# Retiming the loads of the next batch's adjacency matrix in a four-layer graph network

## The chip, the cores and the metric

The kernel runs on one core of one Trainium2 chip. The metric is the device time of one execution in microseconds (us); lower is better. All arithmetic is in 32-bit floats.

## What is computed

Eight independent batches `b`, each with node features `x[b]` (2048 x 128) and an adjacency matrix `adj[b]` (2048 x 2048, 16 MB), pass through four layers. Each layer adds its result to `x`; its input is `h = relu(layernorm(x))`. Cut to what matters:

```
# layer 0: three graph convolutions on h
for i in range(3):
    h = relu(layernorm(adj^T @ (h @ Ws[i]) + bs[i] + h) * gammas[i] + betas[i])
# layer 1: additive attention, softmax over j of sum_d a[d]*relu(q[j,d] + k[i,d]), masked where adj == 0
# layer 2: four-head dot attention, masked by (1 - adj) * -1e9
# layer 3: normalised propagation
A1 = adj + eye(2048);  d = rsqrt(sum(A1, axis=-1))
x = x + ((A1 * d[:, None] * d[None, :]) @ h) @ B
```

Every layer needs the whole of `adj[b]`.

## The kernel before, in words

A batch is cut into 16 tiles of 128 rows; a tile of `adj` is 128 x 2048 floats, 1 MB. Batches are done one after the other, and each in four stages that follow the layers. All engines run their own programs and meet on semaphores.

**Where `adj` lives.** Layer 0 uses it three times, so it is held whole in on-chip memory, in `A` (`adj_res`, line 147), 16 tiles. This memory is the same that layers 1 and 2 use for their own buffers (lines 148 to 165), so `A` of the next batch can only be loaded in the last stage of the batch before, when those buffers are no longer in use. Layers 1, 2 and 3 read `adj` again through a small ring of two tiles, `ring` (`adj_ring`, line 93), one slot for even and one for odd tiles; each tile is loaded anew in each of the three stages. The ring loads are issued by SyncE (line 301), which waits for each slot on `ring_free`.

**Who loads `A`.** POOL does, in `batch(b, more)` (lines 346 to 364), one transfer of 1 MB per tile with line 350, at the head of its program for the batch. Each load of batch b waits on the semaphore `hb_sb` for a tile of the last stage of batch b-1. For batch 0 there is no earlier batch, so ScalarE raises `hb_sb` by 16 at the start (line 493), and all sixteen waits pass. Behind the loads stand the small LayerNorm steps of POOL (`rstd_step`, lines 325 to 332). Tiles 0 to 7 raise `adj_in[0]` and tiles 8 to 15 `adj_in[1]`.

**The last stage (layer 3), lines 1169 to 1197.** TensorE goes through the 16 tiles in eight pairs, 0 to 7. For a pair:

- it transposes both ring tiles in 16 blocks each into PSUM (L1177), after VectorE has added the identity to each tile's diagonal block (`self_loops`, L766), which in turn waits for the ring load;
- ScalarE and VectorE copy the transposed blocks out (L374, L778) into `AGG` and `HT`;
- it multiplies them with `H`, first the even tile, then the odd one (L1189; 32 instructions a tile, since a 32-bit matmul is issued as two). The first of these for each tile raises `ring_free`, and SyncE issues the next pair's load into that slot;
- ScalarE copies each tile's product out (`evac(hbT...)`, line 565), and this raises `hb_sb` by one. That is the event on which the loads of `A` wait;
- a last small matmul (L1197) and an update of `X` (L786) end the pair.

The waits of this cycle that matter in code:

```
1187    pe.wait_ge(o3_rdy, T + (NT + 2))
1191    if j == 0:
1192        last.then_inc(ring_free, 1)
 565    evac(hbT[:, u, :], ps[:, 6 + u, 0:P]).then_inc(hb_sb, 1)
```

So in each pair there are up to four transfers of 1 MB: two into the ring for the next pair, and the loads of `A` released by this pair's two tiles. The last pair has no ring load after it. In the last batch's last stage there is no load of `A` at all.

**The next batch's first stage.** TensorE starts layer 0 with the first half of `A` for all four column chunks (`aggregate`, L1001, 64 instructions), after a wait for `adj_in[0]`, and then takes the second half after a wait for `adj_in[1]` (line 1115). Within the second half it calls `project` (L986), which needs ScalarE's copy of the chunk (`evac_agg`, L374). ScalarE begins the batch with twelve row sums over the tiles of `A` for the degrees (`degrees`, L424), with the same two waits ahead of tile 0 and tile 8 (line 421), and comes to `evac_agg` after them. SyncE first issues the store of the result of the batch before (L305), waits for it, and then issues sixteen loads of 64 KB into `X` (L293) and the first ring load of the batch. `X` is read in the third graph convolution (line 857 and below).

Of the kernel before, what the change touches and what calls it, by code (L numbers as in the profile page):

```python
# [12 lines left out]
NT = N // P  # L13
# [47 lines left out]
def e_lag(u, m):  # L61

    return 2 if u * QUADS + m - TURN in (0, 1) else EQ


class Steps:
# [13 lines left out]
def build(nc, x, adj, Ws, bs, gammas, betas, W1, W2, a_vec, Wq, bq, Wk, bk, Wv, bv, Wo, bo, Bw, out):  # L80
# [4 lines left out]
    with ExitStack() as ctx:  # L85
# [3 lines left out]
        def sem(name):  # L89
            return ctx.enter_context(nc.semaphore(name))  # L90
# [155 lines left out]
        hb_sb = sem("hb_sb")  # L246
# [66 lines left out]
        @block.gpsimd  # L313
        def _(pool):
            pool.memset(ident[:, :], 0.0).then_inc(pool_self, 1)
            pool.memset(halves[:, :], -0.5).then_inc(pool_self, 1)
            pool.memset(epses[:, :], LN_EPS).then_inc(pool_self, 1)
            pool.memset(ones[:, :], 1.0).then_inc(pool_self, 1)
            pool.wait_ge(pool_self, 4)
            pool.affine_select(out=ident[:, :], in_=ident[:, :], compare_op=ALU.not_equal, fill=1.0, base=0,  # L320
                               pattern=[[-1, P]], channel_multiplier=1).then_inc(id_rdy, 1)
            own = Steps(pool_self, LN_COUNT + 1)
            own.k = 4

            def rstd_step(b, k):

                over = LN_STEPS[k][1]
                t = slice(over[0], over[-1] + 1)
                pool.wait_ge(ln_stats, b * LN_COUNT + k + 1)
                own.done(pool.tensor_tensor(var[:, t], mv[:, t, 1], epses[:, t], ALU.add))  # L330
                own.wait(pool, b)
                pool.tensor_tensor(rstd[:, t], var[:, t], halves[:, t], ALU.pow).then_inc(ln_rstd, 1)

            def fetch(b):

                pool.dma_start(HW[:, :].rearrange("p (t d) -> p t d", t=NT),
                               x_v[bass.ds(b, 1)].rearrange("o p t d -> p (o t) d")).then_inc(xn_in, 16)

            def fetched_rstd(b):

                pool.wait_ge(xn_stats, b + 1)
                nc.gpsimd.tensor_tensor(xvar[:, :], xmv[:, :, 1], epses[:, :], ALU.add).then_inc(xvar_rdy, 1)
                pool.wait_ge(xvar_rdy, b + 1)
                nc.gpsimd.tensor_tensor(xrstd[:, :], xvar[:, :], halves[:, :], ALU.pow).then_inc(xn_rstd, 1)

            def batch(b, more):
                own.k = 4
                for t in range(NT):
                    pool.wait_ge(hb_sb, b * NT + t + 1)
                    pool.dma_start(A[:, t, :], adj_v[bass.ds(b, 1), t].rearrange("o p n -> p (o n)")).then_inc(adj_in[t // HALF], 16)  # L350
                for k in range(LN_EARLY):
                    rstd_step(b, k)

                pool.wait_ge(deg_rdy, (b + 1) * NT)
                own.done(pool.tensor_tensor(deg1[:, :], deg[:, :], ones[:, :], ALU.add))
                own.wait(pool, b)
                pool.tensor_tensor(dinv[:, :], deg1[:, :], halves[:, :], ALU.pow).then_inc(dinv_rdy, 1)
                for k in range(LN_EARLY, LN_MID):
                    rstd_step(b, k)
                pool.wait_ge(qk2_dve, b * 2 + 1)  # L360
                fetch(b + 1 if more else b)
                fetched_rstd(b + 1)
                for k in range(LN_MID, LN_COUNT):
                    rstd_step(b, k)

            fetch(0)
            fetched_rstd(0)
            for b in range(NB):
                batch(b, b < NB - 1)

        @block.scalar
        def _(act):
# [61 lines left out]
            def quad(T, m, u, first):  # L434
                if not (first and m < EQ):
                    act.wait_ge(e_used, T * QUADS + (m - e_lag(u, m) + 1))
                s = e_slot(u, m)
                nc.scalar.activation(E[:, s + 2, SPLIT:N], Q2[:, SPLIT:N], ACT.Relu, bias=ka[:, u, 32 + m:33 + m])  # L438
                nc.scalar.activation(E[:, s + 3, :], Q2[:, :], ACT.Relu, bias=ka[:, u, 48 + m:49 + m]).then_inc(e_act, 1)  # L439
# [129 lines left out]
        def _(dve):  # L569
# [104 lines left out]
            def quad(T, m, u, first):  # L674
                if not (first and m < EQ):
                    dve.wait_ge(e_used, T * QUADS + (m - e_lag(u, m) + 1))
                s = e_slot(u, m)
                nc.vector.tensor_scalar(E[:, s, :], Q2[:, :], kd[:, u, m:m + 1], 0.0, ALU.add, ALU.max)  # L678
                nc.vector.tensor_scalar(E[:, s + 1, :], Q2[:, :], kd[:, u, 16 + m:17 + m], 0.0, ALU.add, ALU.max)  # L679
                nc.vector.tensor_scalar(E[:, s + 2, 0:SPLIT], Q2[:, 0:SPLIT], kd[:, u, 32 + m:33 + m], 0.0,  # L680
                                        ALU.add, ALU.max).then_inc(e_dve, 1)
# [538 lines left out]
```

## Time and profile before

| what | value |
|---|---|
| time, median of 3 runs | 13284.21 us (13282.43 to 13297.99) |
| the profiled execution | 13291.54 us |
| its span | 13289.7 us |
| TensorE matmul busy | 12572.4 us, 95% of the span |
| VectorE busy | 9769.1 us, 74% |
| ScalarE busy | 9628.7 us, 72% |
| POOL busy | 351.3 us, 3% |
| mean granted TensorE clock | 0.972 of full speed |
| moved by the DMA engines | 647.66 MB, mean 49 GB/s |
| ring loads | 384 of 1 MB, median 4.9 us from issue to landing |
| loads of `A` | 128 of 1 MB, median 7.4 us |

The span is the time from the first to the last instruction of the profiled execution. An engine's busy time is the union of its instructions. The chain that ended last is found by going back from the last instruction, at each step to what released it; a microsecond saved on an engine counts only where that chain runs through it. A batch takes about 1656 us, of which the last stage is some 100 us.

### The profile page before, as it was taken

The page shows a single profiled execution, that of the slowest core. Times are in us where ns is not written, and L with a number is a line of the kernel's source. Part 1 is how long each engine was busy: PE and PEld are TensorE (multiplying, and loading weights), DVE is VectorE, ACT ScalarE, POOL GpSimd, SP SyncE. Part 2 cuts the span into 40 slices and gives each one's busy share as a digit, 9 for nine tenths or more (in the row PEclk, how much of TensorE's full clock was granted, in tenths as well). Part 3 has the DMA queues.
Part 4 walks back from the last instruction along what each step waited for, and adds up shares of the span by engine and source line. Part 5 has one row for each costly group of instructions (what it writes and reads, how often), then busy time and mean ns, then how long its engine had stood idle before and what let it go on. Part 6 is the DMA issues. An engine that isn't in the chain of part 4 may idle for free.

```text
span 13289.7 us, 251470 instructions
## 1 busy us (share of the span) xinstructions
PE 12572.4 (95%) x110721; PEld 6215.5 (47%) x110721; DVE 9769.1 (74%) x13975; ACT 9628.7 (72%) x8953; POOL 351.3 (3%) x500
## 2 busy tenths in 40 slices
PE   8998999989999899998999989999899998999989
PEld 3333843338433384333843338433384334843348
DVE  4887748877488774887758877588765887658876
ACT  4886748867488664886648866488664886658866
POOL 1000000000000000000000000000000000000000
PEclk9999999999999999999999999999999999999999
DMA  1001210012100121001310013100130001300022
GB/s 71 17 20 45 100 60 17 20 45 104 56 17 20 48 105 52 17 20 48 110 47 18 19 48 117 40 20 17 52 122 32 20 17 52 129 25 20 17 55 87
DMA packets 126941, 647.66 MB, mean 49 GB/s; under 512 B 15264, under 2 KB 49824, under 8 KB 52128
## 3 DMA queue, kind: packets, MB, share of 16 engines
q1 hardware_dynamic: 92688, 420.78, 9.4%
q0 software_dynamic: 20880, 143.66, 2.9%
q10 hardware_dynamic: 12288, 67.13, 2.2%
q8 instruction: 879, 14.40, 0.4%
q14 instruction: 206, 1.69, 0.0%
HBM read 556.01 MB, written 8.39 MB: 42 GB/s over the span
## 4 chain that ended last, share of the span: by engine, by line
PE 88%; DVE 6%; ACTq 2%; DMA 2%; ACT 1%; issue 1%; POOL 0%; SPq 0%; DVEq 0%
PE ps L1017 50%; PE ps L1001 10%; PE ps L1059 8%; PE ps L1072 4%; PE ps L1030 4%; PE ps L1050 3%; PE ps L1189 3%; ACTq L540 2%; PE ps L953 2%; DMA adj_ring<-in_adj 1%; PE ps L1177 1%; DVE E L678 1%; DVE E L679 1%; DVE PT L705 1%; DVE stats L604 1%
## 5 line engine op out<-in xcount | busy, mean ns | idle before, releaser
L1017 PE MATMUL ps<-E,a_win 128*32 128x512 f32 x65536 | 7128.7, 594 | 46.4 <-ACT E L439 34.9
L1017 PEld LDWEIGHTS ps<-E,a_win 128*32 128x32 f32 x65536 | 2114.9, 110 | 4879.7 <-issue 4737.3
L439 ACT ACTIVATE E<-Q,ka 128x2048 f32<-128x2048 f32 x2048 | 4073.1, 1989 | 0.0
L678 DVE TENSOR_SCALAR E<-Q,kd 128x2048 f32<-128x2048 f32 x2048 | 2631.1, 1285 | 1016.5 <-PE ps L1017 982.4
L438 ACT ACTIVATE E<-Q,ka 128x1280 f32<-128x1280 f32 x2048 | 2786.7, 1361 | 810.9 <-PE ps L1017 786.0
L679 DVE TENSOR_SCALAR E<-Q,kd 128x2048 f32<-128x2048 f32 x2048 | 2623.9, 1281 | 0.0
L746 DVE CUSTOM_DVE_ANT_0 T<-ps,adj_ring 128x2048 f32<-128x2048 f32 x512 | 1173.5, 2292 | 231.9 <-PE ps L1050 205.3
L680 DVE TENSOR_SCALAR E<-Q,kd 128x768 f32<-128x768 f32 x2048 | 1258.8, 615 | 0.0
L464 ACT ACTIVATE T<-T,nmin 128x2048 f32<-128x2048 f32 x512 | 1022.0, 1996 | 319.4 <-issue 199.3
L374 ACT ACTIVATE PT<-ps 128x512 f32<-128x512 f32 x1792 | 999.7, 594 | 287.3 <-PE ps L1059 275.4
L1059 PE MATMUL ps<-ident,T 128*128 128x128 f32 x8192 | 1129.8, 281 | 10.1 <-ACT PT L374 5.9
L1059 PEld LDWEIGHTS ps<-ident,T 128*128 128x128 f32 x8192 | 886.3, 142 | 219.2 <-issue 201.2
L374 ACT ACTIVATE AGG<-ps 128x512 f32<-128x512 f32 x224 | 127.7, 596 | 1095.8 <-PE ps L1001 979.7
L1001 PE MATMUL ps<-adj_res,H 128*128 128x512 f32 x2048 | 889.5, 592 | 0.0
L1050 PE MATMUL ps<-kst,qcur 128*128 128x512 f32 x2048 | 624.7, 428 | 267.7 <-DMA kst<-kl 224.5
L1072 PE MATMUL ps<-PT,V 128*32 128x128 f32 x16384 | 658.5, 279 | 0.0
L1001 PEld LDWEIGHTS ps<-adj_res,H 128*128 128x128 f32 x2048 | 384.2, 190 | 459.2 <-issue 459.2
L1030 PEld LDWEIGHTS ps<-H,PT 128*128 128x128 f32 x4096 | 476.8, 195 | 110.6 <-issue 110.6
L1050 PEld LDWEIGHTS ps<-kst,qcur 128*128 128x128 f32 x2048 | 360.4, 197 | 329.1 <-issue 241.9
L1030 PE MATMUL ps<-H,PT 128*128 128x128 f32 x4096 | 501.0, 282 | 7.0 <-DVE PT L705 7.0
L753 DVE COPY PT<-ps 128x512 f32<-128x512 f32 x512 | 353.0, 690 | 178.8 <-PE ps L1059 178.2
L1001 PE MATMUL ps<-adj_res,HW 128*128 128x512 f32 x1024 | 447.3, 595 | 32.5 <-DMA adj_res<-in_adj 32.5
(119 smaller groups left out, 7558.4 us busy)
## 6 DMA issues: line engine op xcount, KB each, us to landing
adj_ring<-in_adj SPq DMA_DIRECT2D x384, 1024.0 KB, 4.9
adj_res<-in_adj POOLq DMA_DIRECT2D x128, 1024.0 KB, 7.4
qst<-qh ACTq DMA_DIRECT2D x64, 256.0 KB, 7.9
qst<-ql ACTq DMA_DIRECT2D x64, 256.0 KB, 9.0
kst<-kh ACTq DMA_DIRECT2D x64, 256.0 KB, 5.7
kst<-kl ACTq DMA_DIRECT2D x64, 256.0 KB, 5.9
HW<-in_x POOLq DMA_DIRECT2D x9, 1024.0 KB, 13.3
X<-in_x SPq DMA_DIRECT2D x128, 64.0 KB, 2.0
```

The source lines that it names most:

```text
L438: nc.scalar.activation(E[:, s + 2, SPLIT:N], Q2[:, SPLIT:N], ACT.Relu, bias=ka[:, u, 32 + m:33 + m])
L439: nc.scalar.activation(E[:, s + 3, :], Q2[:, :], ACT.Relu, bias=ka[:, u, 48 + m:49 + m]).then_inc(e_act, 1)
L678: nc.vector.tensor_scalar(E[:, s, :], Q2[:, :], kd[:, u, m:m + 1], 0.0, ALU.add, ALU.max)
L679: nc.vector.tensor_scalar(E[:, s + 1, :], Q2[:, :], kd[:, u, 16 + m:17 + m], 0.0, ALU.add, ALU.max)
L680: nc.vector.tensor_scalar(E[:, s + 2, 0:SPLIT], Q2[:, 0:SPLIT], kd[:, u, 32 + m:33 + m], 0.0, ALU.add, ALU.max).then_inc(e_dve, 1)
L746: nc.vector.tensor_tensor_reduce(out=T2[:, h, :], in0=ps[:, 0:4, :].rearrange("p c n -> p (c n)"), in1=ring[:, u, :], scale=1.0, scalar=BI ...
L1001: last = mm(ps[:, c, :], src[:, t, :], A[:, t, c * CH:(c + 1) * CH], start=(t == 0), stop=(t == NT - 1))
L1017: last = mm(ps[QROWS * grp:QROWS * (grp + 1), 4 * u + c, :], win, E[:, s + grp, c * CH:(c + 1) * CH], start=(m == 0), stop=(m == QUADS - 1 ...
L1030: last = mm(ps[:, 4 * u, 0:D], PT1[:, j * P:(j + 1) * P], H[:, j, :], start=(j == 0), stop=(j == NT - 1))
L1050: last = mm(ps[:, c, :], qcur[:, u, h, :], kst[:, h, c * CH:(c + 1) * CH], start=True, stop=True)
L1059: last = nc.tensor.transpose(ps[:, 4 + g % 2, k * P:(k + 1) * P], T2[:, h, j * P:(j + 1) * P], ident[:, :])
L1072: last = mm(ps[HD * k:HD * (k + 1), 6 + h % 2, 0:P], V[:, g * TPC + k, h * HD:(h + 1) * HD], PT2[:, g, k * P:(k + 1) * P], start=(g == 0), ...
```

## The change

A table names for each tile `t` of the next batch's `A` the tile of the last stage whose `hb_sb` count releases its load. Before, that was tile `t` itself.

```diff
 def e_lag(u, m):
 
     return 2 if u * QUADS + m - TURN in (0, 1) else EQ
+
+
+LOAD_AFTER = (0, 1, 3, 4, 6, 8, 9, 11, 12, 13, 14, 14, 15, 15, 15, 15)
 
 
 class Steps:
@@ -346,7 +349,7 @@
             def batch(b, more):
                 own.k = 4
                 for t in range(NT):
-                    pool.wait_ge(hb_sb, b * NT + t + 1)
+                    pool.wait_ge(hb_sb, b * NT + LOAD_AFTER[t] + 1)
                     pool.dma_start(A[:, t, :], adj_v[bass.ds(b, 1), t].rearrange("o p n -> p (o n)")).then_inc(adj_in[t // HALF], 16)
                 for k in range(LN_EARLY):
                     rstd_step(b, k)
```

Load 2 now waits for tile 3, load 3 for tile 4, and so on; the six loads 10 to 15 wait for tiles 14, 14, 15, 15, 15 and 15, the tiles of the last pair. Nothing else differs. In the profile of the changed kernel, all line numbers below line 63 are higher by 3.

## Rows read from the trace of the kernel before

**Rows 1.** The page, chain that ended last: shares of the span by line

```profile
PE ps L1017 50%; PE ps L1001 10%; PE ps L1059 8%; PE ps L1072 4%; PE ps L1030 4%; PE ps L1050 3%; PE ps L1189 3%; ACTq L540 2%; PE ps L953 2%; DMA adj_ring<-in_adj 1%; PE ps L1177 1%; DVE E L678 1%; DVE E L679 1%; DVE PT L705 1%; DVE stats L604 1%
```

**Rows 2.** Busy table, the eight last stages: length, engines, PEclk, DMA share, GB/s

```profile
1604.40:1709.10 104.70, 93.66 (x769) 90.95 (x770) 30.47 (x73) 22.54 (x53) 8.29 (x16) 0.95 0.79 289
3262.50:3365.60 103.10, 93.00 (x769) 89.75 (x770) 30.24 (x74) 22.48 (x53) 8.35 (x16) 0.96 0.80 294
4916.70:5022.90 106.20, 96.24 (x769) 93.35 (x770) 30.70 (x73) 22.55 (x53) 8.30 (x16) 0.92 0.78 285
6577.90:6675.60 97.70, 91.01 (x769) 87.79 (x770) 30.15 (x73) 22.34 (x53) 8.31 (x16) 0.98 0.85 310
8230.10:8327.90 97.80, 92.43 (x769) 89.37 (x770) 30.38 (x73) 22.39 (x53) 8.26 (x16) 0.97 0.84 310
9882.30:9986.20 103.90, 93.88 (x769) 90.90 (x770) 30.48 (x73) 22.50 (x53) 8.25 (x16) 0.95 0.80 292
11541.20:11636.80 95.60, 91.11 (x769) 87.77 (x770) 30.22 (x73) 22.33 (x53) 8.32 (x16) 0.98 0.87 317
13188.70:13283.80 95.10, 90.53 (x768) 87.56 (x768) 30.20 (x73) 22.09 (x52) 0.00 (x0) 0.98 0.46 155
```

**Rows 3.** The chain in order of time, last stage of batch 0: start, length, what

```profile
1662.18 10.10 DMA adj_ring<-in_adj
```

**Rows 4.** The same in the last stage of the last batch

```profile
13206.34 6.20 DMA adj_ring<-in_adj
...
13230.64 7.68 DMA adj_ring<-in_adj
```

**Rows 5.** Line 301 in the last stages of batch 0 and of the last batch

```profile
DMA to landing us min/median/max: 4.7/5.1/10.1
...
DMA to landing us min/median/max: 4.7/4.9/7.7
```

**Rows 6.** Busy table by pair, batch 0 (first two) and last batch

```profile
1617.70:1634.60 16.90, 12.61 (x102) 12.18 (x101) 4.50 (x11) 3.14 (x7) 1.06 (x2) 0.93 0.78 299
1646.70:1658.20 11.50, 11.36 (x102) 11.06 (x101) 4.15 (x11) 3.03 (x7) 1.06 (x2) 1.00 0.95 336
...
13215.10:13226.80 11.70, 11.56 (x102) 11.37 (x103) 4.21 (x11) 3.03 (x7) 0.00 (x0) 1.00 0.54 181
13226.80:13240.90 14.10, 11.62 (x102) 10.98 (x100) 4.09 (x11) 3.03 (x7) 0.00 (x0) 1.00 0.43 150
```

**Rows 7.** Busy table at the start of the program, first batch's loads of A

```profile
30.00:40.00 10.00, 0.00 (x0) 0.00 (x0) 0.96 (x2) 0.00 (x0) 2.09 (x5) 1.00 1.01 425
...
60.00:70.00 10.00, 10.00 (x25) 4.45 (x24) 0.00 (x0) 6.31 (x7) 0.00 (x0) 1.00 0.59 246
```

**Rows 8.** DMA queues from 13229 to 13238: packets, MB, share of 16 engines

```profile
q8 instruction: 1, 0.02, 0.7%
```

**Rows 9.** Line 350, whole program: duration ns min/median/max, first and last start

```profile
L350 POOL DMA_DIRECT2D adj_res<-in_adj x128: 530/530/617, 23.6 to 11636.5; - x128
...
DMA to landing us min/median/max: 4.9/7.4/35.3
```

**Rows 10.** Turn from batch 0 to 1: timelines of POOL, SyncE; chain; L424; ScalarE

```profile
1705.28 0.53 POOL L350 DMA_DIRECT2D adj_res<-in_adj  x1 [9.04 <-ACT hbT L374]
1708.86 0.53 POOL L350 DMA_DIRECT2D adj_res<-in_adj  x1 [3.04 <-ACT hbT L374]
...
1709.52 0.40 SPq L305 DMA_DIRECT2D out_x<-X  x1
...
1709.10 36.05 PE ps L1001 x84
...
L424 ACT ACTIVATE adj_ring<-adj_res x12: 1901/1909/1912, 1708.8 to 1731.2; 128x2048 f32<-128x2048 f32 x12
...
1743.48 0.60 ACT L374 ACTIVATE AGG<-ps 128x512 f32<-128x512 f32 x1 [10.29 <-PE ps L1001]
```

**Rows 11.** Timeline of POOL in pair 4 of batch 0's last stage

```profile
1662.54 0.53 POOL L350 DMA_DIRECT2D adj_res<-in_adj  x1 [7.53 <-ACT hbT L374]
```

## The prediction, made before the changed kernel was run

> **What bounds the kernel now.** I read the page's chain of work first. Nine of its fifteen named shares are lines of TensorE, L1017 alone with half of the span; the only transfer of any weight is the ring load, `adj_ring<-in_adj`, at 1% [rows 1]. So the change can touch only short stretches in which the chain leaves TensorE for a ring load. `adj_res`, which the change retimes, is not named there. The first batch's loads are left alone by the change: all their waits are satisfied from the outset.
>
> Second, the busy table over the last stage of each batch, from its first L1189 to the next batch's first L1001 [rows 2]. This is the best view here, because the kernel holds its own control: the last batch has no next one, so its stage runs without any of the sixteen loads of A. It takes 95.1 us with the DMA engines 0.46 busy. The other seven take 95.6 to 106.2 us at 0.78 to 0.87, and add up to 709.0 us (104.7 + 103.1 + 106.2 + 97.7 + 97.8 + 103.9 + 95.6). Seven times 95.1 is 665.7. **43.3 us in the whole program** go with the loads of A, 6.2 us a batch on average, 0.4 to 11.1 in a single one.
>
> Third, the chain inside such a stage. In batch 0 it leaves TensorE three times for a ring load, each issued with the second tile of a pair, at worst for 10.10 us [rows 3]. The same chain in the last batch still leaves twice, for 6.20 and 7.68 us [rows 4]. All fourteen ring loads there land in 4.7 to 7.7 us, median 4.9, and in batch 0 in 4.7 to 10.1, median 5.1 [rows 5]. So a ring load of about 5 us is hidden, each microsecond above it is paid, and the median ring load does not suffer from A; the long ones do.
>
> Fourth, pair by pair [rows 6], each stretch from one pair's first L1189 to the next's: pairs 1 and 3 of batch 0, pairs 2 and 3 of the last. An undisturbed pair takes 11.5 or 11.7 us, whether it moves 336 GB/s (batch 0) or 181 (the last). A disturbed one takes 16.9 with A's loads, 14.1 without. A pair of before asks for two ring loads and two of A, 4 x 1.049 MB = 4.19 MB in 11.5 us, or 365 GB/s; with the first batch's loads in flight the core got 425 GB/s [rows 7]. It runs at 86% of what it can have, so a lagging DMA engine makes up its lag slowly. I take a stall's size as that lag plus what else stands in its queue. What starts it is there without A as well: during the last batch's long ring load, issued at 13230.64, one 16 KB packet of the instruction queue went out [rows 4, 8]. The change does not remove that.
>
> **The change, part by part.** It removes and adds no instruction. The same 128 `adj_res` loads are issued by POOL, 0.53 us each [rows 9]; only the tile whose `hb_sb` count releases each of them moves. Before, two loads go with every pair. After, by pairs 0 to 7: 2, 1, 1, 1, 2, 1, 2, 6. Pairs 0 to 6, in which ring loads are in flight, issue 10 instead of 14.
>
> *Last stage.* Pairs that ask for 4.19 MB fall from seven to three (0, 4 and 6); the other four ask for 3.15 MB, 274 GB/s in 11.5 us, 64% of 425. Sharing the 43.3 us evenly over seven pairs, the four lightened ones give back 4/7, 24.7 us. Pair 0 starts with empty queues and its ring loads seldom stall, so evenly over pairs 1 to 6 it is 4/6, 28.9 us. I take **27 us**, between them. Bounds: 0 if the stalls merely move, 43.3 if the stage becomes that of the last batch; more only where a stage also escapes the stalls that the last batch itself has (14.1 - 11.7 = 2.4 us is one of its two).
>
> *The turn to the next batch.* Now six loads instead of two start at the end. The ones after tile 14 go out where 1705.28 stands and 0.5 us later, the four after tile 15 at 1708.86 to 1710.5 [rows 10]. Loads of A land in 7.4 us median [rows 9]. The first batch's sixteen move at 425 GB/s, and their last ones are still seen between 60 and 70 us [rows 7]: 1.049 MB at 425 GB/s is 2.5 us apiece. An estimate for six: 1705.3, plus up to about 4 us until bytes move, plus 6 x 2.5, plus 2.5 for the result's 1 MB store issued at 1709.5 [rows 10], is 1727. TensorE wants the second half of A after 64 of the 84 L1001 matmuls that run from 1709.10 in 36.05 us, at 1709.1 + 27.5 = 1736.6 [rows 10]: nearly 10 us of cover. ScalarE reaches tile 8 sooner. Its twelve degree sums L424 start between 1708.8 and 1731.2, one in 2.04 us, so it asks for tile 8 at 1725 and would wait some 2 us; after them it idles 10.29 us until the first L374 [rows 10]. That cover takes the wait. Cost taken: nothing. If the cover is gone, each late microsecond is paid seven times.
>
> *What is queued behind the waits.* On POOL, the loads that stay for tile 15 have only the LayerNorm steps of the next batch behind them, which have no input until the first projection, after the 84 matmuls, at 1745 [rows 10]. On SyncE nothing moves; but the sixteen X loads wait for the result's store, and go later by what that store loses to the bunch, at most the 15 us that six loads take. X is read only in the last of three layers, the one ring load behind them after these: and for both I take nothing.
>
> The sum against the profiled execution: 13291.5 - 27 = 13264.5 us. The median of the runs is 7.3 us below that execution, so against it: 13284.2 - 27 = **13257 us**.
>
> **The rivals.**
> *Little gain, 0 to 20 us.* What hurts is not the volume but one load in the wrong place. The load after an even tile is issued 0.4 us behind the second ring load (1662.54 against 1662.18) [rows 3, 11]. Such a load remains in pairs 0, 2, 3, 4 and 6, five of seven, and only pairs 1 and 5 would gain: 2/7 of 43.3 is 12 us, 13272. The Trainium skill, "DMA: Bandwidth & Descriptors", section "Queues, rings and completion order", says that each DMA engine takes turns between the queue rows that have work, packet by packet; by that rule a single load of A alongside is enough to slow a ring load, and this rival would hold. Against it: the pair at 1646.7 has both loads of A and takes 11.5 us [rows 6], and the median ring load of batch 0 is 0.2 us above the last batch's [rows 5].
>
> *All of it, 35 to 50 us.* With a quarter of the volume gone from pairs 1, 2, 3 and 5 the queues drain each time, and only the stalls that the last batch also has are left: 13284.2 - 43.3 = 13241. For it: two of the seven stages (95.6, 97.7) are near the control even with all fourteen loads [rows 2]. Against it: two neighbouring full or half-full spots remain (pairs 4 to 6).
>
> *Slower: the bunch at the turn comes late.* Its place is `adj_in[1]`, before TensorE's second half and ScalarE's ninth degree sum. The loads' landings bound it: from 4.9 us after issue up to 35.3, the slowest of the first sixteen [rows 9]. At the upper end the last lands at 1710.5 + 35.3 = 1745.8, TensorE waits 9.2 us, seven times 64 us, less 27: 13321. It decides from 27/7 = 3.9 us of wait, so from a last landing 31 us after the first L1001. Against it: the sixteen had a queue nearly three times as long as six, and the estimate above has the last landing at 1727.
>
> That the change doesn't do what it says is hardly possible: POOL issues in order and the sixteen wait values never fall, so no load is held up by an earlier one's later release.
>
> **How the numbers follow.** 0.2% is 26.6 us, about what a measurement of this kernel can tell from no change. The forecast case (gain 20 to 35, 0.55) lies across that mark: half of it counts as faster, half as the same. Everything (0.17) is faster, little gain (0.21) the same, the late bunch (0.07) slower. Faster 0.27 + 0.17, rounded with the runs' own spread to 0.46; same 0.47; slower 0.07. The range reaches from 50 us of gain to none, 13234 to 13284, with 2 us above for the runs' spread; outside it lie the late bunch and the edges.
>
> **What would show it.** In the changed profile, the seven last stages should add up to about 680 us, with pairs 1, 2, 3 and 5 near 11.7 us and what stalls remain sitting after pairs 0, 4 and 6. Ring loads at the median stay at 4.9 us, and fewer take over 8. L1001 has no wait on `adj_res` beyond the first batch's; ScalarE's L424 waits for it some seven times for a few microseconds, and the idle time ahead of L374 at the turn shrinks from 10.3 us by as much. Wrong it would be if stalls stayed as many and as long in pairs 2 and 3 (little gain), or if L1001 waited for `adj_res` at every turn.

## The result, and the profile after

| | before | after |
|---|---|---|
| median of 9 runs each | 13297.99 us (13282.43 to 13309.64) | 13245.61 us (13235.77 to 13249.89) |
| ratio, 95% interval | | 0.9961 (0.9950 to 0.9971) |
| span of the profiled execution | 13289.7 us | 13239.4 us |
| the seven last stages that can have loads of `A` | 709.0 us | 663.8 us |

The kernel is faster by 0.39%. The forecast was 27 us off 13284, which is 13257, with a chance of 0.46 for faster and 0.47 for no difference. The measured median lies 11 us below it and inside the range. The gain itself is 52.4 us between the medians and 50.3 us between the two profiled executions, almost double the forecast one: the kernel before had come out at 13284 in three runs and at 13298 in nine, and that shift hides half of the miss. Line numbers are higher by 3: L1177, L1189, L1001 are now L1180, L1192, L1004.

The chain that ended last, by line, from the profile's page, to set against [rows 1]. The ring load has moved behind L1180 and the two L681/L682 groups; by engine, the same page gives DMA 1% of the chain instead of 2%.

```profile
PE ps L1020 50%; PE ps L1004 10%; PE ps L1062 8%; PE ps L1075 4%; PE ps L1033 4%; PE ps L1053 3%; PE ps L1192 3%; ACTq L543 2%; PE ps L956 2%; PE ps L1180 1%; DVE E L681 1%; DVE E L682 1%; DMA adj_ring<-in_adj 1%; DVE PT L708 1%; DVE stats L607 1%
```

The busy table over the same eight last stages as [rows 2], with the same columns: length; PE, PEld, DVE, ACT, POOL busy; granted clock, DMA share, GB/s.

```profile
1607.60:1705.40 97.80, 92.73 (x769) 90.44 (x770) 30.58 (x73) 22.42 (x53) 6.66 (x13) 0.95 0.74 267
3258.30:3353.10 94.80, 91.18 (x769) 87.84 (x770) 30.11 (x74) 22.38 (x53) 6.73 (x13) 0.98 0.77 275
4903.80:4998.00 94.20, 90.76 (x769) 87.77 (x770) 30.14 (x73) 22.29 (x53) 6.65 (x13) 0.98 0.77 277
6552.30:6646.50 94.20, 90.25 (x769) 87.64 (x770) 30.12 (x73) 22.30 (x53) 6.63 (x13) 0.98 0.78 277
8200.10:8296.10 96.00, 91.14 (x769) 87.84 (x770) 29.98 (x74) 22.36 (x53) 6.71 (x13) 0.98 0.77 272
9848.70:9943.10 94.40, 89.75 (x769) 87.77 (x770) 30.56 (x73) 22.32 (x53) 6.66 (x13) 0.98 0.78 276
11497.10:11589.50 92.40, 90.16 (x769) 87.71 (x770) 30.20 (x73) 22.30 (x53) 6.66 (x13) 0.98 0.78 282
13141.80:13233.50 91.70, 90.42 (x768) 88.35 (x768) 30.41 (x73) 22.09 (x52) 0.00 (x0) 0.97 0.47 161
```

Three things are to be seen. The first seven are all shorter and much more alike: 92.4 to 97.8 us where they were 95.6 to 106.2. They still move 267 to 282 GB/s, with ten of the loads of `A` beside the ring loads. And the last stage, which has no load of `A` in either kernel, went from 95.1 to 91.7 us by itself: 3.4 us that the change can't have caused, and a warning about the control of [rows 2].

Who waited for whom in the changed kernel: us in total, times, longest.

```profile
ACT adj_ring L427 <- DMA adj_res<-in_adj: 25.5, 5, 19.1
PE ps L1180 <- DVE adj_ring L769: 58.9, 21, 5.3
PE ps L1004 <- DMA adj_res<-in_adj: 33.1, 1, 33.1
```

The middle line is the ring's stalls as TensorE feels them. The kernel before had 91.0 us there, in 35 waits; 32 us are gone. The median ring load takes 4.9 us in both kernels, as forecast. The first and third show the turn: TensorE waits for `adj_res` once, at the program's start, and ScalarE five times, of which two at the start make 22.7 us and three at turns 2.8. So the six loads of the last pair cost nothing. The turn itself, batch 0 to 1, against [rows 10] (the chain; SyncE's timeline; landings of line 353 from 1700 to 1710):

```profile
1705.41 36.05 PE ps L1004 x84
...
1705.83 0.40 SPq L308 DMA_DIRECT2D out_x<-X  x1
1722.70 7.45 SPq L296 DMA_DIRECT2D X<-in_x  x16
...
DMA to landing us min/median/max: 5.2/8.1/13.7
```

The last of the six is issued at 1706.7, so all have landed by 1720.4, 15 us after the first L1004; TensorE asks 27.5 us after it. The X loads go out 17.3 us after the first L1004, 9.0 us before the change, and nobody waits for them.

The groups of TensorE's lines in the stage, out<-in, count, busy and mean ns, idle before: first the kernel before, then the changed one.

```profile
L1177 PE MATMUL ps<-ident,adj_ring 128*128 128x128 f32 x2048 | 266.4, 291 | 91.1 <-DVE adj_ring L766 91.0
```

```profile
L1180 PE MATMUL ps<-ident,adj_ring 128*128 128x128 f32 x2048 | 254.0, 284 | 58.9 <-DVE adj_ring L769 58.9
```

The same 2048 transposes became 12.4 us shorter in busy time. After a long wait TensorE's granted clock is lower for a while: in the pair at 1617.7, with a ring load of 9.7 us for which TensorE sat idle for 4.15 us, it was 0.93 on average over its two levels, 1.2 and 2.4 GHz, and in the undisturbed one at 1646.7 it was 1.00 [rows 6]. A stall is paid a little over its own length.

### The profile page after: what moved, and what is told of

Its sections match the earlier page's. It is cut to its first block, busy times and chain, and to the rows that moved or that the text cites. A ratio compares the mean times of both kernels' runs of the same rounds, so it can differ in the third digit from the quotient of the medians.

```text
span 13239.4 us, 251470 instructions
## 1 busy us (share of the span) xinstructions
PE 12548.4 (95%) x110721; PEld 6198.5 (47%) x110721; DVE 9763.9 (74%) x13975; ACT 9628.5 (73%) x8953; POOL 350.6 (3%) x500
## 4 chain that ended last, share of the span: by engine, by line
PE 89%; DVE 6%; ACTq 2%; DMA 1%; ACT 1%; issue 1%; POOL 0%; SPq 0%; DVEq 0%
PE ps L1020 50%; PE ps L1004 10%; PE ps L1062 8%; PE ps L1075 4%; PE ps L1033 4%; PE ps L1053 3%; PE ps L1192 3%; ACTq L543 2%; PE ps L956 2%; PE ps L1180 1%; DVE E L681 1%; DVE E L682 1%; DMA adj_ring<-in_adj 1%; DVE PT L708 1%; DVE stats L607 1%
## 5 line engine op out<-in xcount | busy, mean ns | idle before, releaser
L681 DVE TENSOR_SCALAR E<-Q,kd 128x2048 f32<-128x2048 f32 x2048 | 2628.6, 1284 | 1018.6 <-PE ps L1020 983.2
L682 DVE TENSOR_SCALAR E<-Q,kd 128x2048 f32<-128x2048 f32 x2048 | 2620.8, 1280 | 0.0
L1004 PE MATMUL ps<-adj_res,H 128*128 128x512 f32 x2048 | 889.5, 592 | 0.0
L1004 PEld LDWEIGHTS ps<-adj_res,H 128*128 128x128 f32 x2048 | 384.2, 190 | 459.2 <-issue 459.2
L1004 PE MATMUL ps<-adj_res,HW 128*128 128x512 f32 x1024 | 447.7, 595 | 33.1 <-DMA adj_res<-in_adj 33.1
```

The costliest lines, as they stand in the source:

```text
L1004: last = mm(ps[:, c, :], src[:, t, :], A[:, t, c * CH:(c + 1) * CH], start=(t == 0), stop=(t == NT - 1))
```

## The experiments

All variants are compared with runs of the kernel before on the same chip. "Seven stages" is the sum, over batches 0 to 6 of the profiled execution, of the time from the first L1192 to the first L1004 of the next batch (where loads behind the last tile make L1004 wait, to the end of L1200, where it could have started). Nine of the twelve differ from the changed kernel in the table only.

| run | loads of `A` by pairs 0 to 7 | ratio (95%) | seven stages | TensorE's waits for the ring |
|---|---|---|---|---|
| before / again | 2 2 2 2 2 2 2 2, one behind each tile | 0.9998 (0.9990 to 1.0007) | 709.0 / 706.4 | 91.0 / 92.2 |
| e12 | 2 2 2 2 2 0 0 6, one behind each tile | 0.9986 (0.9977 to 0.9994) | 692.9 | 80.1 |
| e5 | 2 2 2 1 2 1 2 4, one behind a tile | 0.9979 (0.9969 to 0.9989) | 685.6 | 74.1 |
| e2 | 2 2 2 2 2 2 2 2, both behind the odd tile | 0.9983 (0.9974 to 0.9992) | 681.7 | 67.7 |
| e4 | 2 1 1 1 2 1 2 6, all odd | 0.9962 (0.9950 to 0.9975) | 674.0 | 64.5 |
| e3 | 2 1 1 1 2 1 2 6, all even | 0.9959 (0.9945 to 0.9973) | 669.3 | 58.9 |
| after / again | 2 1 1 1 2 1 2 6 | 0.9961 / 0.9962 | 663.8 / 669.3 | 58.9 / 63.1 |
| e9 | 2 2 2 2 2 2 2 2, both behind the even tile | 0.9960 (0.9947 to 0.9972) | 667.4 | 62.4 |
| e10 | 2 1 1 1 1 1 1 8, all even | 0.9957 (0.9944 to 0.9971) | 661.8 | 58.2 |
| e6 | 2 1 1 1 2 1 0 8 | 0.9963 (0.9950 to 0.9975) | 660.8 | 57.2 |
| e7 | 0 0 0 0 0 0 0 16 | 1.0098 (1.0084 to 1.0112) | 645.6 | 49.5 |
| e11 | as e7, more instructions on POOL | 1.0242 (1.0228 to 1.0256) | 651.3 | 52.0 |

### The two kernels again

`e1` is the kernel before, unchanged.

> The kernel before, unchanged, to learn how far its time and its last stages move by themselves. Both theories: ratio 1.000 within 0.1%; the seven stages with loads of A add up to about 709 us as in the first profile, give or take 10, and the last one lies between the 95.1 us seen before the change and the 91.7 us seen after it.

`e8` is the changed kernel, unchanged.

> The changed kernel once more, on the chip of its variants: ratio 0.996, seven stages at 664 us give or take 8.

Measured: 0.9998 and 0.9962, the seven stages 706.4 and 669.3 us. All three expected figures of the stages were met. The last stage of `e1` took 92.4 us, not 95.1. What lies outside the eight last stages (span less stages) was 12485.5 and 12480.6 us before, 12483.8 and 12494.3 after: it moves by more than 10 us by itself, so a single pair of spans can't price this change to better than that. The stages can, to some 5 us (the changed kernel's two profiles differ by 5.5): 37 and 45 us.

### How much without any load

```diff
-LOAD_AFTER = (0, 1, 3, 4, 6, 8, 9, 11, 12, 13, 14, 14, 15, 15, 15, 15)
+LOAD_AFTER = (15,) * 16
```

> All sixteen loads behind the last tile, so that no last stage has any beside its ring loads: eight samples of the control. Stage: each of the eight takes 91 to 96 us, the seven add up to about 655 us, with stalls of 1 to 3 us left where a packet of the instruction queue falls beside a ring load (both theories). Turn: TensorE waits some 24 us for the first eight at each of seven turns, about 170 us in all, so the ratio is 1.008 to 1.010.

The stages came to 645.6 us, below the expected 655, a floor with seven samples. It also agrees with the last stage alone: over the fourteen profiles it took 90.5 to 95.1 us, 92.3 on average, and seven times that is 646 us. **The 95.1 us of the kernel before were the highest of fourteen.** The whole price of the loads in the stage was thus 709.0 and 706.4 less 646, 63 and 60 us, not 43.

The turn cost what was worked out (batch 5 to 6; chain, then TensorE's timeline):

```profile
10067.59 20.80 DMA adj_res<-in_adj
...
10088.43 7.03 PE L1004 MATMUL ps<-adj_res,HW 128*128 128x512 f32 x10 [24.35 <-DMA adj_res<-in_adj]
```

### Volume or place

```diff
 # e2: both behind the odd tile
+LOAD_AFTER = (1, 1, 3, 3, 5, 5, 7, 7, 9, 9, 11, 11, 13, 13, 15, 15)
 # e9: both behind the even tile
+LOAD_AFTER = (0, 0, 2, 2, 4, 4, 6, 6, 8, 8, 10, 10, 12, 12, 14, 14)
 # e3, e4: the changed kernel's count, all even, all odd
+LOAD_AFTER = (0, 0, 2, 4, 6, 8, 8, 10, 12, 12, 14, 14, 15, 15, 15, 15)
+LOAD_AFTER = (1, 1, 3, 5, 7, 9, 9, 11, 13, 13, 14, 14, 15, 15, 15, 15)
```

> Two loads of A per pair as before, but both released by the pair's odd tile, none by the even one. Volume theory (a stall's size is a lag that a queue at 86% of its rate cannot work off): nothing gained, ratio 0.999 to 1.001, the seven stages near 709 us. Position theory (the load issued 0.4 us behind the second ring load does the harm): most of the gain of the change, ratio 0.996 to 0.997, the stages near 670 us.

> The changed kernel's count of loads in every pair (2, 1, 1, 1, 2, 1, 2, 6), but every one in pairs 0 to 6 released by the even tile. Volume theory: same as the changed kernel, ratio 0.996. Position theory: the gain is mostly lost, ratio 0.998 to 1.000, more than 0.1% slower than the kernel with all of them behind the odd tile.

> The same count in every pair, every load in pairs 0 to 6 released by the odd tile. Volume theory: as the changed kernel, ratio 0.996. Position theory: faster than it, ratio 0.995, the seven stages near 645 us, with hardly a ring load over 7 us.

`e2` missed both: 681.7 us, 0.9983, between "nothing" (709) and "most of it" (670). The gain at an unchanged volume, though, was already too much for the volume theory. `e3` and `e4` came out alike, 669.3 and 674.0 us, as that theory wanted and the position theory did not. So one more was needed, the other half of `e2`:

> Two loads of A per pair as before, both released by the even tile. Two behind the odd tile made the seven stages 681.7 us against 706.4 and 709.0 with one behind each tile. If it is the odd tile's place that helps, this one gives nothing, 705 us or more and a ratio near 1.000. If it helps that two loads go out back to back and leave the rest of the pair free, this one gives the same as the odd one: 675 to 690 us, ratio 0.998.

It gave 667.4 us and 0.9960: **the whole gain of the change, with all fourteen loads still in pairs 0 to 6.** That was more than either alternative said, and both theories fall: the volume isn't what the change gained by, and the load behind the even tile, which the rival accused, stands in the better place (the intervals of `e9` and `e2` are apart). The fourteen loads aren't free even there: `e9` lies 21 us above the floor. Batch 6, the best of its seven stages, had no stall (busy table, columns as above):

```profile
11495.90:11587.20 91.30, 89.94 (x769) 87.75 (x770) 30.36 (x73) 22.31 (x53) 8.53 (x16) 0.98 0.89 332
```

332 GB/s for 91.3 us, more than any stage of the kernel before, and as short as a stage without loads. The other six took 93.9 to 98.5 us, with nine late ring loads among them, ones that the chain waits for.

What the place does is seen in the DMA queues (packets, MB, share of 16 engines; q0 carries POOL's loads, q1 SyncE's). First `e9`, pair starting at 11544.19, two loads issued at 11548.6: the first 4 us behind the issue, then the next 5.

```profile
q1 hardware_dynamic: 160, 1.07, 81.4%
q0 software_dynamic: 13, 0.11, 6.4%
...
q0 software_dynamic: 272, 1.98, 93.8%
q1 hardware_dynamic: 14, 0.09, 12.5%
```

These two loads of `A` begin to move some 4 us after their issue. By then the pair's second ring load is nearly through, and by the end of the second stretch 1.98 of their 2.10 MB have followed, just as the packets of the next pair's first ring load, issued at 11556.4, come up. The 4 us aren't a delay of POOL's own. Here are the first 2 us behind the issue of such a pair of loads, first in `e9` (11548.6 to 11550.6), then in `e2` (11554.9 to 11556.9):

```profile
q1 hardware_dynamic: 60, 0.36, 73.5%
q8 instruction: 1, 0.02, 2.8%
```

```profile
q0 software_dynamic: 17, 0.14, 54.0%
q1 hardware_dynamic: 27, 0.09, 11.1%
```

In `e9` no packet of q0 is among them. Over all fourteen profiles, a load of `A` that had no other one in flight sent its first packet 3.5 to 4.0 us after its issue where a ring load had been issued 0.35 us before it, 2.3 to 2.5 us where that was 1.6 or 1.7 us before, and 1.2 to 1.3 us where it was 3.9 us or more, or where no ring load was under way, but for two loads of `e6` (below). So it waits until the ring load ahead has been served. A load behind the odd tile is issued 3.6 us later and begins 1.2 us after that; taken over all pairs, 95 in 100 packets of `A` have gone 9.1 us after the issue of the pair's second ring load in `e9`, 10.0 us in the kernel before and 10.8 us in `e2` (medians), and the next pair's first ring load is issued after some 8 us. The same view for the 3 us that follow the issue of a pair's first ring load, in the kernel before (1658.6 to 1661.6), in `e2` (11559.4 to 11562.4) and in `e9` (11556.4 to 11559.4):

```profile
q0 software_dynamic: 124, 0.88, 69.3%
q1 hardware_dynamic: 38, 0.31, 30.9%
```

```profile
q0 software_dynamic: 158, 1.04, 83.0%
q1 hardware_dynamic: 24, 0.20, 17.6%
```

```profile
q1 hardware_dynamic: 71, 0.58, 64.9%
q0 software_dynamic: 63, 0.39, 30.6%
```

In the kernel before the ring load gets a third of the engines at first, and behind its second ring load comes the even tile's load as well, so a pair's two ring loads have `A` on both sides, and so on into the next pair. In `e2` they have it only in front, and the stalls are as many (26 pieces of the chain against 25) but smaller, 6.5 us a ring load against 7.4. In `e9` they have it hardly at all, and 9 pieces are left. In the seven stages of all fourteen profiles the ring load that the chain waits for is always the second one that a pair issues, never the first. That the place of the loads makes the gain is shown by these runs; how a load of `A` ahead of the first ring load makes the second one late is not.

### In a row, or apart

```diff
 # e5: twelve and four
+LOAD_AFTER = (0, 1, 2, 3, 4, 5, 7, 8, 9, 11, 12, 13, 14, 14, 15, 15)
 # e12: the late six without the spreading
+LOAD_AFTER = (0, 1, 2, 3, 4, 5, 6, 7, 8, 9, 14, 14, 15, 15, 15, 15)
```

> Twelve loads of A in pairs 0 to 6 and four in the last pair, between before (14 and 2) and after (10 and 6). Volume theory: half of the gain, ratio 0.998, the seven stages near 687 us. Position theory: even-tile loads stand in six of the seven pairs as against five after and seven before, so also about half. It gives the slope for the volume.

> One part of the change without the other: ten loads in the stage and six in the last pair, as in the changed kernel, but the ten stay one behind each of the tiles 0 to 9, so pairs 0 to 4 are as before and pairs 5 and 6 have none. If only the number of loads counts: as the changed kernel, ratio 0.996, the seven stages near 667 us. If what counts is how many pairs in a row have a load behind each tile (7 of 7: 708 us, 5 of 7 in the kernel with twelve: 686, 3 separate ones in the changed kernel: 667): about 5/7 of the 61 us above the floor of 646 stay, near 690 us, ratio 0.998 to 0.9985.

`e5` gave 685.6 us and 0.9979, half of the gain. The rival's expectation had miscounted: its table has loads behind even tiles in five pairs (0, 1, 2, 4, 6), not in six, as many as the changed kernel, so the rival called for as much gain here as there, and half of it speaks against the rival too. `e12` is the one that separates the change's two parts: the last six loads are late as in the changed kernel, the first ten are not spread. It kept 692.9 us, and its ratio of 0.9986 is apart from the changed kernel's 0.9961, with no overlap of the intervals. So **putting six loads behind the last pair is worth about a third of the gain; the spreading is the rest**: some 16 us of the 45 (709.0 - 692.9) are there without it. The two parts were taken in this order only, and `e9` shows that the whole gain can also be had without the late six, so they aren't shares that add up in every table. The excess over 646 goes with the pairs that have a load behind each of their tiles: seven of them 60 to 63 us, five in a row 47, five in groups of three, one and one 40, three apart 18 to 23, none 21 to 23 with all on even tiles (`e9`, `e3`) and 28 to 36 with all on odd ones (`e4`, `e2`). Three apart cost nothing over none. Whether five in a row are worse than five in groups, 7 us, can't be told from the 5.5 us by which the changed kernel's two profiles differ.

### How late the last loads may be

```diff
 # e6: eight behind the last tile
+LOAD_AFTER = (0, 1, 3, 4, 6, 8, 9, 11, 15, 15, 15, 15, 15, 15, 15, 15)
 # e10: eight in the stage, all even, two behind tile 14, six behind tile 15
+LOAD_AFTER = (0, 0, 2, 4, 6, 8, 10, 12, 14, 14, 15, 15, 15, 15, 15, 15)
```

> Eight loads in pairs 0 to 6 and eight behind the last tile. Volume theory: the seven stages gain some 5 us more in all, to about 659 us. The turn: eight landings at 2.5 us each from about 4 us after the last tile end some 24 us after the first L1004, against 27.5 us when TensorE wants them, so TensorE does not wait; ScalarE waits some 8 us and has 10.3 us to spare. Ratio 0.995 to 0.996. If the late bunch decides instead, TensorE waits for adj_res at every turn and the ratio is above 0.997.

> Eight loads in pairs 0 to 6 (two in pair 0, one in each other), all on the even tile, two behind tile 14 and six behind tile 15. Volume theory: the seven stages come to 655 to 665 us, half-way from the changed kernel (664 and 669) to the floor without loads (646). The turn: two of the eight start 3.6 us earlier than in the kernel with eight behind the last tile, so TensorE does not wait. Ratio 0.995 to 0.9965. Rival: the stage is at its floor and the ratio stays at 0.996.

With eight behind the last tile the cover is used up, a little sooner than worked out: the last landing was expected after 24 of the 27.5 us and no wait of TensorE. Waits of `e6`:

```profile
ACT adj_ring L427 <- DMA adj_res<-in_adj: 91.9, 9, 19.1
PE ps L1004 <- DMA adj_res<-in_adj: 35.5, 3, 33.1
```

TensorE waited in two of seven turns, 2.4 us in all; ScalarE some 10 us at each, all of it covered. In just these two turns, batches 2 to 3 and 5 to 6, POOL issued its loads 0.6 us behind SyncE's store of the result, and they sent their first packet 4.6 us after that instead of 1.2 us. In `e10` TensorE waited in no turn, as expected. Both kernels have the stages at 660.8 and 661.8 us, which can't be told from the changed kernel's 663.8 and 669.3, and neither has a ratio that is apart from the change's. `e10` has the lowest ratio of all, 0.9957; that it beats the changed kernel is not shown.

### What starts a stall

```diff
                 own.k = 4
+                for pair in range(NT // 2 - 1 if b else 0):
+                    pool.wait_ge(hb_sb, b * NT + 2 * pair + 1)
+                    for _ in range(256):
+                        pool.wait_ge(hb_sb, 1)
                 for t in range(NT):
```

> As the kernel with all sixteen loads behind the last tile, but POOL, idle in the stage, runs 256 more waits that are already satisfied in each of pairs 0 to 6 of batches 0 to 6, 16 KB of instructions a pair that have to be fetched. Theory that a packet of the instruction queue starts the stalls: more of them fall beside a ring load, and the seven stages rise from 646 us to 652 to 665. Rival (the stalls have another cause): the stages stay at 643 to 649 us. TensorE's wait at the turn stays 24 us.

The stages came to 651.3 us, between the rival's 643 to 649 and the theory's 652 to 665, so this figure decides nothing: it is 5.7 us above `e7`, and the changed kernel's two profiles differ by 5.5. The extra packets are there, 49 of them, 255 against 206, but of 8 KB each, half of the 16 KB expected for a pair (`e11`, then `e7`; the queue's packets, MB and share):

```profile
q14 instruction: 255, 2.09, 0.0%
```

```profile
q14 instruction: 206, 1.69, 0.0%
```

The 1792 waits of a stage are 896 instructions in the trace, two waits in each. They took some 118 us, 17 us for a pair of 11.5, so POOL ran behind and its loads went out 30 us late at each turn, which is all of the 1.4% more. The late ring loads speak more clearly than the total: `e11` has eight in its seven stages and `e7` five, and only two of the eight have a q14 packet beside them. So there is no sign that POOL's instruction packets, 8 KB on queue q14, start stalls, though a small effect isn't excluded.

It doesn't clear q8, whose 16 KB packets carry the bulk of the program's instructions: of the twelve stalls left in the changed kernel's seven stages, eleven have a q8 packet between 1.7 us before and 3.3 us after the issue of the ring load that is late, while only some six such packets come in a stage of 95 us, so that a third would be expected by chance. The same count over all fourteen profiles: of 215 late ring loads, 138 have such a packet, 64%; of the 471 second ring loads of a pair that weren't late, 80 have one, 17%. And it splits the stalls in two. The kernel before has, in its two profiles, 26 stalls with a packet and 23 without; the changed kernel 21 and 6; `e9` in its one 7 and 2; `e7`, with no load of `A` in the stage, 4 and 1. What the change removed is mostly the stalls without a packet. The worst one left (chain, then the queues from 1637 to 1640):

```profile
1637.38 9.06 DMA adj_ring<-in_adj
```

```profile
q8 instruction: 1, 0.02, 1.9%
```

That is a coincidence in time, not a cause shown. No run takes q8's packets away, so it stays open what starts the stalls that are left.

## Why the prediction was right, and where it was not

**Right: where the time is.** Ring loads that come late, each microsecond above about 5 us paid, a floor with two ring loads a pair, all in the seven last stages. The stages moved by 45 us and 37 us, the rest of the program by nothing that stands out of its own 10 us.

**Right: the turn costs nothing.** The last landing was put at 1727, or 18 us after the first L1001 [rows 10]; it came no later than 15 us after. ScalarE waited in three turns of seven, 2.8 us in all, where some 2 us in each of seven were expected. Eight loads used the cover up in two turns of seven (`e6`), where 2.5 us a load had left 3.5 us of it. The late bunch was no danger with six. Its bound from the first sixteen loads was far off, as the smaller queue let expect.

**Wrong in size: "43.3 us in the whole program".** The term was the difference to one stage, [rows 2, last row], taken for the control. That sample was the longest of fourteen; the floor is 646 us and the term 60 to 63, not 43.3. With 61.5 in its place the step's own fractions, 4/7 and 4/6, give 35 to 41 us, and 37 and 45 were measured. That it came out so well is luck, as the next point shows. The view had a hint: two of its seven disturbed stages (95.6, 97.7) were nearly as short as the undisturbed one, which the prediction read as luck of those two and not as bad luck of the control.

**Wrong in its reason: "pairs that ask for 4.19 MB".** The sum shared the gain out by volume. At full volume `e9` has the whole gain, so 365 of 425 GB/s is not too much; it is when the loads move. Counting the pairs with four transfers gave the right fraction only because in this table the same pairs, 0, 4 and 6, are the ones with a load behind each tile. `e9` and `e2` have seven pairs with four transfers and 667.4 and 681.7 us. Nor did the gain arise in the pairs that were lightened. Two profiles of each kernel have, by the pair in which the late ring load is issued, from 0 to 6, 1, 12, 5, 8, 8, 6 and 9 stalls before and 1, 10, 4, 0, 1, 10 and 1 after: pairs 1, 2, 3 and 5, which lost a load, went from 31 to 24, and pairs 0, 4 and 6, which kept both, from 18 to 3.

**The rival of little gain fell too.** It blamed the load behind the even tile. It took packet-by-packet turns between queues from the Trainium skill ("DMA: Bandwidth & Descriptors", "Queues, rings and completion order"). This trace doesn't show them with the packets that it counts, of 8 KB: the even tile's load has no packet for 3.5 us or more while the ring load ahead of it moves. No run tells whether a packet of the skill's is one of these or several. What the rival had wrong is that it took the issue time, 0.4 us behind the second ring load, for the time of moving. The load moves 3.7 us after its issue, when the ring loads are done. The pair at 1646.7, which the prediction held against the rival, showed it.

**The stages' total.** Forecast "about 680", measured 664 and 669. Ring loads above 8 us fell from five to two in the chains of the seven stages. The stalls that remain were forecast for pairs 0, 4 and 6 and sit in pairs 1, 2 and 5. Twenty of the 27 in the two profiles are in pairs 1 and 5, the ones that come right after pairs 0 and 4 with their load behind each tile (pair 6 is followed by the last pair, which has no ring load). `e6`, with the same pairs 0 and 4, has 9 of 14 there, `e4`, with both loads behind the odd tile, 13 of 17; `e3`, with both behind the even tile, only 4 of 14. It is the pair that follows which pays.

## What to carry to other kernels

Before a transfer is moved, find in the DMA queues when it moves, not when it is issued, and put it where the urgent transfers leave a gap; here fourteen loads a batch, two back to back in each gap, cost 21 us in the program, and one behind each tile cost 60. A stretch of the same program without the suspect is a good control, but one sample is not: where stalls are a matter of coincidence, take several, or make a kernel that gives them. A table that spreads work and delays part of it is two changes; run each alone.

## What was not expected of the hardware

- A load of `A` issued 0.35 us behind a ring load sent its first packet 3.5 to 4.0 us after its issue; with the last ring load 3.9 us old or more, or none under way, the same load began after 1.2 to 1.3 us.
- In the seven stages of the fourteen profiles every stall is of the second ring load that a pair issues. Of these stalls, 64% have a 16 KB instruction packet beside them, against 17% of the second ring loads that weren't late.
- With two loads behind each even tile the core drew 332 GB/s beside undisturbed matmuls, at a DMA share of 0.89, with no stall in one whole stage (batch 6 of `e9`).
- A stall lengthens the work behind it: 2048 transposes took 266.4 us of TensorE in the kernel before and 254.0 in the changed one, and 251.2 in `e7`.
